# A scan layer and an expert layer on one core: one interleaved loop, or two phases

## The chip, the cores and the metric

The kernel runs on one core of a Trainium2 chip. A core has TensorE (PE, matrix products into PSUM), VectorE (DVE), ScalarE (ACT), GpSimd (POOL) and SyncE (SP, which issues transfers). SBUF is the working memory, PSUM has eight banks of 128 x 512 f32. The metric is the device time of the program in microseconds, the median of several runs. The profile is one further execution.

## What is computed

Input is 16 sequences of 512 tokens with 128 features. Four sublayers follow one another, each with a residual and a layer norm: linear attention, a first expert layer, a state-space layer, and a second expert layer. The change touches the last two only. Cut from the reference:

```python
xz = x @ in_proj_w.T                       # 128 -> 512, split into xi, z of 256
xc = silu(conv4(xi) + conv_b)              # depthwise, 4 taps
xp = xc @ x_proj_w.T                       # dt_raw, B (16), C (16)
dt = softplus(dt_raw * dt_proj_w + dt_proj_b)
dA = exp(dt * A); dBx = dt * xc * B        # for each of 16 states
h_t = dA_t * h_(t-1) + dBx_t               # scan over 512 tokens
y  = sum_n h[n] * C[n] + xc * D
x3 = layernorm(x2 + (y * silu(z)) @ out_proj_w.T)
# second expert layer: 8 experts of 176, top 2, and a shared one, computed densely
h  = silu((x3 @ w1 + b1) * (x3 @ w3 + b3)) * gate
out = layernorm(x3 + h @ w2 + biases)
```

## The kernel before

Stage 1 (attention and routing), the choice of tokens and the first expert layer fill the time up to about 503 us. They are the same in both kernels. After that comes one loop in which every engine runs the same `iteration(f, s, m, o, ahead)`, written out in steps n = 0 to 15, one for each state. Four sequences are in it at a time: `s` is being scanned, `f` (the next one) is being prepared by `front` (normalisation x2, transposition, convolution, projections, softplus), and `m` and `o` (the two before) are in the expert layer, one chunk of 128 hidden units in each step, 13 chunks in all.

A sequence has its 256 channels as two halves of 128 partitions (`NH` = 2), each with 512 tokens, so that a tile of a state is 128 x 1024. For state n:

- TensorE spreads row B of state n over all partitions (`spread_b`, L890), ScalarE copies it to SBUF (`copy_b`, tile bs, L670), and GpSimd multiplies it by u = dt * xc (`spread_u`, tile dbx, L528).
- ScalarE writes the decays (`scan_step`, tile dA, L678), in two SBUF buffers.
- VectorE runs the scan over both halves in one instruction (tile hst, L1330; the first decay of each half is zero) and multiplies by row C, which TensorE has spread into PSUM (`spread_c`, L894; tile prod, L1343).
- TensorE adds the product into PSUM by a product with the identity (`add_state`, L906). For three pairs of states (PAIRS) VectorE adds two products first (L1348).

At the end of a sequence comes yd (the term with D), y2 (the gate), `out_proj` (L949), x3p (the sum with x2) and the normalisation to x3. In the expert part, TensorE runs `hidden` (w1 and w3, L915 and L917), `spread_w` (gates, L922) and `down` (w2, L934); ScalarE makes ha and ht; VectorE hg, hs and hh (`gate`, `silu`, `weigh`).

The order on each engine is the order in which these functions write it. An engine executes in that order, and waits on semaphores: for instance `bb_rdy` counts the spreads of B, `scan_rdy` the scans, `op_mm` the output projections. `s.at(per, k)` is the count that is reached when k of a sequence's `per` events are done.

## Time and profile before

| | |
|---|---|
| median of 3 runs | 2514.21 us (2509.17 to 2514.93) |
| span of the profiled execution | 2515.7 us |
| VectorE busy | 2154.8 us (86%) |
| TensorE busy | 1786.1 us (71%), mean granted clock 0.844 |
| GpSimd busy | 1118.2 us (44%) |
| ScalarE busy | 1035.9 us (41%) |
| first scan starts | 551.64 us |

The span is from the first to the last instruction; it is 1.5 us above the median of the runs. The granted clock is TensorE's, 1.0 being 2.4 GHz and 0.5 being 1.2 GHz. Busy shares are means over stages: the loop is the part from 503 us.

### The profile page before, as it was taken

The numbers are of one execution on the slowest core, as the hardware profiler recorded it, in microseconds if no ns is written. First come the engines' busy times: TensorE is split into PE (matmuls) and PEld (weight loads), VectorE is DVE, ScalarE is ACT, GpSimd is POOL, SyncE is SP. The second block draws the span as 40 slices with busy tenths as digits, with TensorE's granted clock in tenths as the row PEclk, the third lists the DMA queues.
The fourth block names the chain that finished last, engine by engine and source line by source line (L and its number), as shares of the span: only waits on it lengthen the run. The fifth ranks groups of instructions, "written<-read, shape, count | busy, mean of one in ns | idle before, by whom it ended". The sixth has DMA issues, their size and how long they took to land.

```text
span 2515.7 us, 24789 instructions
## 1 busy us (share of the span) xinstructions
PE 1786.1 (71%) x6433; PEld 982.1 (39%) x6433; DVE 2154.8 (86%) x3132; ACT 1035.9 (41%) x1722; POOL 1118.2 (44%) x602
## 2 busy tenths in 40 slices
PE   4776104346787887877787878787878787878687
PEld 3454003312344444444344434443444444444344
DVE  4888791139899998999999999999999999999996
ACT  1322000135463545454545444454545354636343
POOL 1101306724556454554455545555454445454540
PEclk7999555567898889898898888898888889989899
DMA  6333102300000000000000000000000000000000
GB/s 168 100 106 98 27 1 39 37 17 8 5 5 9 5 9 5 8 4 9 5 9 4 9 5 9 4 13 1 13 0 13 1 13 0 13 1 5 5 1 9
DMA packets 72565, 49.75 MB, mean 20 GB/s; under 512 B 5296, under 2 KB 68432, under 8 KB 72144
## 3 DMA queue, kind: packets, MB, share of 16 engines
q1 hardware_dynamic: 57872, 39.85, 5.5%
q0 software_dynamic: 14592, 8.92, 2.8%
q14 instruction: 82, 0.67, 0.1%
q8 instruction: 19, 0.31, 0.1%
HBM read 27.50 MB, written 21.18 MB: 19 GB/s over the span
## 4 chain that ended last, share of the span: by engine, by line
DVE 35%; PE 26%; issue 22%; POOL 11%; ACT 2%; DMA 1%; SPq 1%; DVEq 1%; POOLq 0%; ACTq 0%
DVE hst L1330 8%; PE bank L906 7%; DVE prod L1343 5%; POOL dbx L528 5%; PE bank L915 3%; PE bank L917 3%; DVE prod L1348 3%; DVE hg L1253 3%; PE bank L934 2%; DVE hh L1266 2%; PE bank L949 1%; DVE cand L1154 1%; DVE val L1157 1%; POOL rwp L506 1%; PE bank L862 1%
## 5 line engine op out<-in xcount | busy, mean ns | idle before, releaser
L528 POOL TENSOR_TENSOR dbx<-u,bs 128x1024 f32<-128x1024 f32 x256 | 719.0, 2818 | 363.9 <-ACT bs L670 232.1
L1330 DVE TENSOR_TENSOR_SCAN hst<-dA,dbx 128x1024 f32<-128x1024 f32 x256 | 675.7, 2639 | 26.2 <-issue 14.6
L906 PE MATMUL bank<-prod,ident 128*128 128x512 f32 x832 | 490.3, 720 | 79.3 <-DVE prod L1348 58.0
L678 ACT ACTIVATE dA<-dt,aneg 128x511 f32<-128x511 f32 x512 | 338.2, 709 | 17.3 <-DVE hst L1330 15.2
L1343 DVE TENSOR_TENSOR prod<-hst,bank 128x1024 f32<-128x1024 f32 x256 | 310.4, 1213 | 19.4 <-PE bank L894 11.2
L670 ACT ACTIVATE bs<-bank 128x512 f32<-128x512 f32 x256 | 151.3, 591 | 338.2 <-PE bank L890 335.4
L906 PEld LDWEIGHTS bank<-prod,ident 128*128 128x128 f32 x832 | 183.3, 226 | 258.3 <-issue 154.7
L691 ACT ACTIVATE ht<-hg 128x512 f32<-128x512 f32 (+1 forms) x208 | 130.8, 629 | 309.5 <-DVE hg L1253 308.3
L915 PE MATMUL bank<-x3T,w_w 128*128 128x512 f32 (+1 forms) x416 | 230.1, 636 | 0.7 <-ACT x3T L696 0.7
L894 PE MATMUL bank<-parts,sel_bc 99*128 99x512 bf16 x256 | 107.6, 420 | 166.0 <-DVE prod L1343 164.2
L917 PE MATMUL bank<-x3T,w_w 128*128 128x512 f32 (+1 forms) x416 | 213.9, 596 | 0.1
L1260 DVE SCALAR_TENSOR_TENSOR hs<-ht,hg 128x512 f32<-128x512 f32 (+1 forms) x208 | 198.7, 955 | 3.9 <-ACT ht L691 2.6
L934 PEld LDWEIGHTS bank<-w_w,hh 128*128 128x128 f32 x1408 | 183.9, 191 | 45.6 <-issue 38.4
L1253 DVE SCALAR_TENSOR_TENSOR hg<-bank,w_b,ha 128x512 f32<-128x512 f32 (+1 forms) x208 | 154.4, 742 | 50.3 <-PE bank L917 50.0
L427 POOL TENSOR_SCALAR rs<-mv 128x4 f32<-128x4 f32 x48 | 51.8, 1079 | 327.1 <-DVE mv L1061 327.1
L934 PE MATMUL bank<-w_w,hh 128*128 128x128 f32 x1408 | 185.8, 275 | 0.8 <-DVE hh L1266 0.8
L685 ACT ACTIVATE ha<-bank,w_b 128x512 f32<-128x512 f32 (+1 forms) x208 | 142.4, 684 | 58.7 <-PE bank L915 57.1
L862 PE MATMUL bank<-x2T,inc 128*128 128x512 f32 x256 | 147.9, 720 | 2.3 <-ACT cv L636 1.4
L917 PEld LDWEIGHTS bank<-x3T,w_w 128*128 128x128 f32 (+1 forms) x416 | 79.5, 191 | 112.2 <-issue 110.3
L1266 DVE TENSOR_TENSOR hh<-hs,bank 128x512 f32<-128x512 f32 x176 | 118.5, 673 | 0.0
L915 PEld LDWEIGHTS bank<-x3T,w_w 128*128 128x128 f32 (+1 forms) x416 | 84.3, 208 | 87.1 <-issue 74.6
L890 PE MATMUL bank<-parts,sel_bc 99*128 99x512 bf16 x256 | 111.4, 435 | 8.7 <-ACT bs L670 7.0
(202 smaller groups left out, 2529.6 us busy)
## 6 DMA issues: line engine op xcount, KB each, us to landing
xg_rows<-xg SPq DMA_DIRECT2D x16, 320.0 KB, 2.5
xt<-in_x SPq DMA_DIRECT2D x16, 256.0 KB, 3.1
xT<-in_xT SPq DMA_DIRECT2D x16, 256.0 KB, 3.4
resid_rows<-zero SPq DMA_DIRECT2D x16, 256.0 KB, 3.4
resid_rows<-resid SPq DMA_DIRECT2D x16, 256.0 KB, 2.4
rin<-resid_rows SPq DMA_DIRECT2D x16, 256.0 KB, 2.8
rin<-resid_rows POOLq DMA_DIRECT2D x16, 256.0 KB, 4.8
out_dram<-ofin SPq DMA_DIRECT2D x16, 256.0 KB, 2.4
```

The costliest lines, as they stand in the source:

```text
L528: gp.tensor_tensor(dbx[n % 2][:, :, :], u[s.par][:, :, :], bs[n % 2][:, :].rearrange("p (h t) -> p h t", h=1).to_broadcast([P, NH, SEQ]), ...
L678: act.activation(dA[n % 2][:, h, 1:SEQ], dt_[s.par][:, h, 1:SEQ], ACT.Exp, scale=aneg[:, h, n:n + 1]).then_inc(da_rdy, 1)
L862: last = mm(pv_ps[:, :], inc[:, k, tile(h)], x2T[:, k:k + SEQ], start=(k == 0), stop=(k == DCONV - 1))
L906: last = mm(y_ps[:, h, :], ident[:, :], prod[n % 2][:, h, :], start=(sums_to(n) == 1), stop=(n == NS - 1), skip_group_check=True)
L915: mm(h1_ps[0:k, :], wt["w1"][:, c, 0:k], x3T[:, :], start=True, stop=True).then_inc(h1_mm, 1)
L917: mm(h3_ps[0:k, :], wt["w3"][:, c, 0:k], x3T[:, :], start=True, stop=True).then_inc(h3_mm, 1)
L934: last = mm(fo_ps[:, tile(q)], h[0:k, tile(q)], wt["w2"][0:k, c, :], start=(c == 0 and q == 0), stop=False, skip_group_check=True)
L1253: stt(hg[c % 2][0:k, :], h3_ps[0:k, :], wt["b3"][0:k, c:c + 1], ha[0:k, :], ALU.add, ALU.mult).then_inc(hg_rdy, 1)
L1260: stt(hs[c % 2][0:k, :], ht[c % 2][0:k, :], 1.0, hg[c % 2][0:k, :], ALU.add, ALU.mult).then_inc(hs_rdy, 1)
L1266: tt(hh[c % 2][:, :], hs[c % 2][:, :], pv_ps[:, :], ALU.mult).then_inc(hh_rdy, 1)
L1330: dve.tensor_tensor_scan(flat(hst[n % 2]), flat(dA[n % 2]), flat(dbx[n % 2]), 0.0, ALU.mult, ALU.add).then_inc(scan_rdy, 1)
L1343: tt(prod[n % 2][:, :, :], hst[n % 2][:, :, :], over_h(cb_ps), ALU.mult).then_inc(prod_rdy, 1)
```

## The change

The loop is cut into two. In the first, `iteration(f, s, m, ahead)` has no expert layer: it scans `s`, prepares `f` and closes `m`, and stores x3 of every sequence to DRAM. When all 16 are stored, the second, `experts(nx, s, pv, ahead)`, loads x3 again and runs the 13 chunks of `s` with the routing of `nx` and the end of `pv`. In the first phase, further:

- The decays are written to PSUM, a bank for each half (`da_ps`), and each half has its own scan. On ScalarE `copy_b` and `front` now stand ahead of the decays.
- The normalisations x2 and x3 are ScalarE's (`Identity` with scale and bias for each token); GpSimd computes scale and shift in four operations instead of two.
- The bias of the convolution, the term with D and the residual x2 are added in PSUM by products with a diagonal matrix or the identity; the pairs are gone, so that all 16 states are added by TensorE. xc, zs and y2 are made by VectorE straight from PSUM; the copies cv and zc are gone.
- The softplus sum and the split of xp into three bf16 parts move from VectorE to GpSimd.

In the second phase ha, h1, h3, the gates' bank and ofin are doubled.

```diff
-            def iteration(f, s, m, o, ahead):        # ScalarE
-                    if m and c >= 1:
-                        chunk_t(m, c - 1)
-                    if s and n < NS - 1:
-                        scan_step(s, n + 1)
-                    if s and n < NS - 2:
-                        copy_b(s, n + 2)
+            def decay(s, n):
+                if n == 0:
+                    act.wait_ge(dt_rdy, s.at(1, 1))
+                for h in range(NH):
+                    need(act, scan_rdy, s.at(NS * NH, NH * (n - 1) + h + 1))
+                    act.activation(da_ps[h][:, 1:SEQ], dt_[s.par][:, h, 1:SEQ], ACT.Exp, scale=aneg[:, h, n:n + 1]
+                                   ).then_inc(da_rdy, 1)
+            def iteration(f, s, m, ahead):
+                for n in range(NS):
+                    if s and n < NS - 2:
+                        copy_b(s, n + 2)
+                    if f:
+                        front(f, n)
+                    if m and n == 3:
+                        act.wait_ge(m_rs, m.at(4, 4))
+                        for k in range(TT):
+                            act.activation(x3o[m.par][:, k, :], blk4(pc_ps)[:, k, :], ACT.Identity, ...
+                    if s and n < NS - 1:
+                        decay(s, n + 1)
...
             def front(s, n):                         # ScalarE
+                if n == 0:
+                    act.wait_ge(f_rs, s.at(4, 4))
+                    need(act, op_mm, s.at(1, -1))
+                    for k in range(TT):
+                        act.activation(x2[s.par][:, k, :], rin[s.par][:, k, :], ACT.Identity, bias=nm1[:, k:k + 1],
+                                       scale=rs1[:, k:k + 1]).then_inc(x2_rdy, 1)
...
+            def skip_term(s):                        # TensorE, step 1
+                need(pe, y2_rdy, s.at(1))
+                for h in range(NH):
+                    mm(y_ps[:, h, :], dskip[:, h, :], xc[s.par][:, h, :], start=True, stop=False, skip_group_check=True)
...
+                    if s:                            # VectorE
+                        dve.wait_ge(dbx_rdy, s.at(NS, n + 1))
+                        for h in range(NH):
+                            dve.wait_ge(da_rdy, s.at(NS * NH, NH * n + h + 1))
+                            dve.tensor_tensor_scan(hst[n % 2][:, h, :], da_ps[h][:, :], dbx[n % 2][:, h, :], 0.0, ALU.mult,
+                                                   ALU.add).then_inc(scan_rdy, 1)
...
+            def experts(nx, s, pv, ahead):           # TensorE
+                for c in range(NCH):
+                    if s:
+                        hidden(s, c)
+                    if pv and c < 2:
+                        down(pv, NCH - 2 + c)
+                    if s and c >= SH_CH:
+                        spread_w(s, c)
+                    if s and c >= 2:
+                        down(s, c - 2)
+                    if nx:
+                        prepare(nx, c)
```

On ScalarE, at the start of a sequence (steps 0 and 1 of the repeated part), before: dA is the decay, bs the copy of B, ht and ha the experts' tiles.

```order
L691 ACTIVATE ht0<-hg0 128x512 [waits hs_rdy]
L678 ACTIVATE dA1<-dt0,aneg 128x511 [waits scan_rdy]
L678 ACTIVATE dA1<-dt0,aneg 128x511
L670 ACTIVATE bs0<-bank2 128x512 [waits dbx_rdy]
L685 ACTIVATE ha<-bank4,w_b1 128x512 [waits hg_rdy,h1_mm]
L691 ACTIVATE ht1<-hg1 128x512 [waits hs_rdy]
L678 ACTIVATE dA0<-dt0,aneg 128x511 [waits scan_rdy]
L678 ACTIVATE dA0<-dt0,aneg 128x511
L670 ACTIVATE bs1<-bank2 128x512 [waits dbx_rdy]
```

The same place of the changed kernel: bank2 and bank3 hold the decays, x2_1 is the next sequence's normalised input.

```order
L743 ACTIVATE bs0<-bank5 128x512 [waits dbx_rdy]
L700 ACTIVATE x2_1<-rin1,nm1,rs1 128x128 [waits op_mm]
L700 ACTIVATE x2_1<-rin1,nm1,rs1 128x128 x3
L750 ACTIVATE bank2<-dt0,aneg 128x511 [waits scan_rdy]
L750 ACTIVATE bank3<-dt0,aneg 128x511 [waits scan_rdy]
L743 ACTIVATE bs1<-bank5 128x512 [waits dbx_rdy]
L750 ACTIVATE bank2<-dt0,aneg 128x511 [waits scan_rdy]
L750 ACTIVATE bank3<-dt0,aneg 128x511 [waits scan_rdy]
```

The copy and the normalisation, which waits for `op_mm`, now stand ahead of the decays, and the experts' tiles are gone from here.

On TensorE, steps 1 and 2 of the changed kernel: bank01 is y, bank5 the spread of B, bank4 that of C, bank7 the output projection, bank6 the transposition and the convolution.

```order
L975 MATMUL bank4<-parts0,sel_bc 128x512 [waits prod_rdy]
L980 MATMUL bank01<-xc0,dskip 128x512 [waits y2_rdy]
L985 MATMUL bank01<-prod0,ident 128x512 [waits prod_rdy]
L971 MATMUL bank5<-parts0,sel_bc 128x512 [waits bs_rdy]
L992 MATMUL bank7<-x2_1,ident 128x512 [waits parts_rdy,y2_rdy]
L996 MATMUL bank7<-w_outp,y2 128x128 x8
L932 MATMUL bank6<-ident,x2_1 128x128 [waits dta_rdy]
L932 MATMUL bank6<-ident,x2_1 128x128 x3
L975 MATMUL bank4<-parts0,sel_bc 128x512 [waits prod_rdy]
L985 MATMUL bank01<-prod1,ident 128x512 [waits prod_rdy]
L971 MATMUL bank5<-parts0,sel_bc 128x512 [waits bs_rdy]
L943 MATMUL bank6<-x2T,inc 128x512 x4
```

In the kernel before, the same steps held an expert chunk each; the skip term and the product with x2 were sums on VectorE.

## Rows read from the trace of the kernel before

**Rows 1.** Windows: length, busy us of PE, PEld, DVE, ACT, POOL (instructions), clock, DMA share, GB/s.

```profile
1244.00:1468.00 224.00, 178.32 (x623) 95.80 (x621) 212.54 (x262) 110.05 (x179) 112.91 (x54) 0.88 0.04 7
...
626.00:642.00 16.00, 9.89 (x17) 3.38 (x18) 14.25 (x15) 9.88 (x14) 11.30 (x4) 0.73 0.00 1
...
2482.00:2504.00 22.00, 22.00 (x103) 13.62 (x101) 15.75 (x24) 10.01 (x16) 0.00 (x0) 1.00 0.00 0
```

**Rows 2.** Time line of VectorE (start us, us): the sum `of`, two sequences apart.

```profile
1036.00 0.68 DVE L1315 TENSOR_TENSOR of<-bank,x 128x512 f32<-128x512 f32 x1
...
1279.41 0.68 DVE L1315 TENSOR_TENSOR of<-bank,x 128x512 f32<-128x512 f32 x1
```

**Rows 3.** Groups by line (busy, mean ns, idle before), and instructions' ns min/median/max.

```profile
L1330 DVE TENSOR_TENSOR_SCAN hst<-dA,dbx 128x1024 f32<-128x1024 f32 x256 | 675.7, 2639 | 26.2 <-issue 14.6 <-POOL dbx L528 10.5
...
L1266 DVE TENSOR_TENSOR hh<-hs,bank 128x512 f32<-128x512 f32 x176 | 118.5, 673 | 0.0
...
L1330 DVE TENSOR_TENSOR_SCAN hst<-dA,dbx x256: 2257/2284/4454, 551.6 to 2439.3; 128x1024 f32<-128x1024 f32 x128
...
L1343 DVE TENSOR_TENSOR prod<-hst,bank x256: 1203/1210/1223, 554.0 to 2442.1; 128x1024 f32<-128x1024 f32 x128
```

**Rows 4.** Time lines of VectorE and GpSimd, a scan beside a dbx.

```profile
562.73 3.48 DVE L1330 TENSOR_TENSOR_SCAN hst<-dA,dbx 128x1024 f32<-128x1024 f32 x1
...
561.70 2.36 POOL L528 TENSOR_TENSOR dbx<-u,bs 128x1024 f32<-128x1024 f32 x1 [2.30 <-DVE hst L1330]
```

**Rows 5.** Time line of TensorE, one step at full clock (two records for one f32 product).

```profile
584.78 0.38 PE L894 MATMUL bank<-parts,sel_bc 99*128 99x512 bf16 x1
585.00 1.88 PE L906 MATMUL bank<-prod,ident 128*128 128x512 f32 x4
586.72 0.38 PE L890 MATMUL bank<-parts,sel_bc 99*128 99x512 bf16 x1
```

**Rows 6.** The same at half clock.

```profile
600.59 3.62 PE L906 MATMUL bank<-prod,ident 128*128 128x512 f32 x4
604.00 0.63 PE L890 MATMUL bank<-parts,sel_bc 99*128 99x512 bf16 x1
```

**Rows 7.** TensorE, output projection and the spread behind it.

```profile
1259.92 2.05 PE L949 MATMUL bank<-w_outp,y 128*128 128x128 f32 x16 [2.49 <-DVE hh L1266]
1261.81 0.38 PE L894 MATMUL bank<-parts,sel_bc 99*128 99x512 bf16 x1
```

**Rows 8.** ScalarE: copy and decays in the time line, then groups by line.

```profile
587.13 0.60 ACT L670 ACTIVATE bs<-bank 128x512 f32<-128x512 f32 x1 [2.06 <-PE bank L890]
...
590.01 1.33 ACT L678 ACTIVATE dA<-dt,aneg 128x511 f32<-128x511 f32 x2
...
L665 ACT ACT_TABLE_LOAD x16 | 20.5, 1283 | 0.3
...
L665 ACT ACTIVATE dta<-dta 128x1024 f32<-128x1024 f32 x16 | 16.9, 1057 | 0.2
```

**Rows 9.** TensorE, one chunk of the last sequence, with no scan beside it.

```profile
2484.15 1.02 PE L915 MATMUL bank<-x3T,w_w 128*128 128x512 f32 x2
...
2486.09 1.05 PE L934 MATMUL bank<-w_w,hh 128*128 128x128 f32 x8
2486.98 1.02 PE L915 MATMUL bank<-x3T,w_w 128*128 128x512 f32 x2
```

**Rows 10.** Routing of the last sequence: VectorE's first reduction, TensorE behind GpSimd's split.

```profile
2467.72 0.17 DVE L1289 TENSOR_REDUCE l1z<-l1e 128x4 f32<-128x32 f32 x1
...
2472.39 0.42 PE L969 MATMUL bank<-identb,rwp 128*96 128x128 bf16 x4 [3.40 <-POOL rwp L513]
```

**Rows 11.** VectorE: the first scan, and the last silu.

```profile
551.64 2.29 DVE L1330 TENSOR_TENSOR_SCAN hst<-dA,dbx 128x1024 f32<-128x1024 f32 x1 [3.57 <-POOL dbx L528]
...
2504.57 0.69 DVE L1260 SCALAR_TENSOR_TENSOR hs<-ht,hg 128x512 f32<-128x512 f32 x1
```

More of the change, by code:

```diff
@@ L69, in need @@
     eng.wait_ge(sem, value)
-def sums_to(n):
-    return n + 1 - sum(a < n for a in PAIRS)
 def schedule(eng, iteration):
@@ L564, in _ @@
+            schedule(gp, experts)
         @block.scalar
@@ L869, in front @@
-                if n == 8:
-                    pe.wait_ge(xc_rdy, s.at(1, 1))
-                    turn(pa_ps, xpf_rdy, s.at(1, 1))
+                    else:
+                        need(pe, x3_rdy, s.at(TT, -TT))
+                    to = (pb_ps, pc_ps)[h]
+                    mm(to[:, :], cbias[:, h, :], ones[:, :], start=True, stop=False)
+                    for k in range(DCONV):
+                        last = mm(to[:, :], inc[:, k, tile(h)], x2T[:, k:k + SEQ], start=False, stop=(k == DCONV - 1))
@@ L907, in add_state, with out_proj @@
                               skip_group_check=True)
                 last.then_inc(y_mm, 1)
+            def out_proj(s):
+                pe.wait_ge(y2_rdy, s.at(1, 1))
+                need(pe, parts_rdy, s.at(1, 1))
+                mm(pc_ps[:, :], ident[:, :], x2[s.par][:, :, :].rearrange("p t d -> p (t d)"), start=True, stop=False,
+                   skip_group_check=True)
+                for k in range(TT):
+                    for h in range(NH):
+                        last = mm(pc_ps[:, tile(k)], y2[:, h, tile(k)], wt["outp"][:, h, :], start=False,
+                                  stop=(h == NH - 1), skip_group_check=True)
+                last.then_inc(op_mm, 1)
@@ new lines, in iteration @@
+            def iteration(f, s, m, ahead):
+                for n in range(NS):
+                    if s:
+                        spread_c(s, n)
+                    if m and n == 0:
+                        add_state(m, NS - 1)
+                    if s and n == 1:
+                        skip_term(s)
+                    if s and n:
+                        add_state(s, n - 1)
+                    if s and n < NS - 2:
+                        spread_b(s, n + 2)
+                    if f and n >= NS - 2:
+                        spread_b(f, n + 2 - NS)
+                    if m and n == 1:
+                        out_proj(m)
+                    if f:
+                        front(f, n)
@@ L1030, in _, with experts @@
[L1030 to L1034 removed]
+            def experts(nx, s, pv, ahead):
+                for c in range(NCH):
+                    if s:
+                        hidden(s, c)
+                    if pv and c < 2:
+                        down(pv, NCH - 2 + c)
+                    if pv and c == 1:
+                        biases(pv)
+                    if s and c >= SH_CH:
+                        spread_w(s, c)
+                    if s and c >= 2:
+                        down(s, c - 2)
+                    if nx:
+                        prepare(nx, c)
@@ L1037, in _ @@
+            for done in st_x3:
+                pe.wait_ge(done, ST_ALL)
+            schedule(pe, experts)
         @block.vector
@@ L1366, in _, with experts @@
-            dve.wait_ge(added, E0 // 2 * 16)
-            dve.wait_ge(added2, E0 // 2 * 16)
+                if c == 4:
+                    need(dve, st_o[s.par], s.half(16))
+                    normalise(ofin[s.par], of, mv3, rs3, s, o_rs, ofin_rdy)
+            def experts(nx, s, pv, ahead):
+                for c in range(NCH):
+                    if pv and c == 0:
+                        silu(pv, NCH - 1)
+                        weigh(pv, NCH - 1)
+                    if s:
+                        gate(s, c)
+                        if c:
+                            silu(s, c - 1)
+                        if c - 1 >= SH_CH:
+                            weigh(s, c - 1)
+                    if pv:
+                        finish(pv, c)
+                    if nx:
+                        prepare(nx, c)
```

781 lines of the change are left out of this document (364 added, 417 removed).

## The prediction

> **What bounds the kernel now.** I read the windows first, then the groups by line, then the time lines of all five engines through one sequence. A sequence takes (1279.41 - 1036.00) / 2 = 121.7 us in steady state [rows 2], and in a window of almost two of them VectorE is busy 95% of the time, TensorE 80% at a granted clock of 0.88, ScalarE and GpSimd half [rows 1]. So VectorE is the bound. Part of its time isn't work: a scan of 1024 elements takes 2.26 us at best and 2.64 in the mean [rows 3], and the pair in [rows 4] shows why: GpSimd's dbx runs from 561.70 to 564.06, the scan issued at 562.73 takes 3.48, that is the 1.33 that dbx still needs and a scan. A product that reads PSUM never does this (1.20 to 1.22 over all 256) [rows 3].
>
> **What the change takes from VectorE.** The decays go to PSUM, so the scan has only one SBUF input, as the product has. I take two half scans at the product's behaviour: the fixed part of an instruction is about 0.14 (2 x 0.67 - 1.21, [rows 3]), so a half scan takes 1.21. With the overlap of 0.08 and the drain before a dependent product, a step is 1.13 + 1.24 + 1.14 = 3.51 us. Sixteen are 56.2; the gating and four halves for xc and zs bring it to about 60, before statistics. No trace row has a scan that reads PSUM; if it kept today's mean, a step would be 3.9. The Trainium skill, SBUF — State Buffer, "SBUF: two separate sides", says that a VectorE instruction with two SBUF inputs and a GpSimd instruction take one port pair in turn, for the whole instruction; by that, 0.36 x 256 = 92 us would come back. The trace agrees with the lock, but I don't book the gain, since VectorE isn't the bound of the new first phase.
>
> **What it puts on the path there.** Prices at full clock [rows 5]: a spread 0.22, adding a state (two f32 products of 512 columns, 0.86 each) 1.72; at half clock adding a state is 3.41 [rows 6]. ScalarE starts the copy bs 0.41 after the spread; it takes 0.60, or 0.50 with the next behind it, and a decay half 0.71 [rows 5, 8]. ScalarE's new order is copy_b(n+2), front(n), decay(n+1), and copy_b(n+2) waits for a spread that stands on TensorE behind adding state n-1. So scan(n+1) can't start before product(n-1) ended plus 0.06 + 0.22 + 1.72 + 0.41 + 0.50 + 0.71 + 0.06 = 3.7 us plus what front(n) costs ScalarE. Before, the decays went ahead of the copy into two SBUF buffers, and this path didn't exist. Against 3.5 of VectorE, a plain step is about even; every front operation now shows.
>
> Walked through all 16 steps of a steady period at full clock, the start of each scan against 3.51 after the last:
> Step 1, the largest. ScalarE's first front work, x2 of the next sequence, waits for op_mm of the sequence before (x2 has two buffers), and decay(1) stands behind it. From the end of product(0): gating 1.2 with its latency, skip term 1.72 (0.1 later), state 0 1.72, spread 0.22, the x2 product 0.86 and out_proj 1.89 [rows 7], latency 0.15, four small ACTIVATEs 1.2 (my estimate, from 0.60 for 512 elements), decay 0.71: 9.7 to 9.8 us in which VectorE does the gating only. +9.7.
> Steps 2 to 6. Statistics 1.5. A convolution half is now five products, 4.3 us, on TensorE ahead of the next step's spread_c; xc waits for a tanh queued behind copy_b; z waits for xc; the four x3 ACTIVATEs stand ahead of decay(4). My walk gives +2.8, +5.3, +0.7, +3.0, +1.6 = 13.4.
> Steps 7 to 12. Fronts of 0.2 to 1.35. A front in two neighbouring steps counts once, as the path spans two steps: +3.2.
> Step 13. Two table loads of 1.28 around Ln of 1.06 [rows 8], now ahead of the decay: +3.1. Step 14: statistics, +1.5.
> GpSimd takes over the softplus sum and the split. It has 16 dbx of 2.36 without a wait for the lock [rows 4], u and the sum at the same price, and about ten small operations, some 50 us in all; the sum stands behind Ln in its queue, with dbx(15), u and the next dbx(0) behind it, and by the walk the last of these ends 1 us before its scan is due. The transfers of x3 lie beside the scans. Both at nothing.
> Sum 56.2 + 30.9 = 87.1 us per sequence at full clock. TensorE works 52 of it (16 x 2.16, 1.7, 8.6, 1.7, 2.8, 1.8, 1), with idle of up to 4 us in steps 1, 2 and 14. The stretch of before without experts, 626 to 642, was granted 0.73, a mixture of 1.2 and 2.4 GHz, with the same bursts and gaps [rows 1]. At 1.2 GHz the path of a plain step is 5.8 (adding 3.41, 0.43 more for the two spreads), and as it spans two steps, it costs 4.7 a step instead of 3.6, 1.1 more. I take half of steps 7 to 15 at that clock (+5): 92 us; bounds 87 (never) and 98 (always there, and one convolution).
>
> **The expert phase.** TensorE bounds it: a chunk takes 2.83 us at clock 1.00, its down part 0.89 [rows 1, 9], while VectorE needs three instructions of 0.67 to 0.74. 26 products of 0.86, 13 of 0.89, 11 of 0.22, and biases, transposes and gates of 2.4 make 38.8. Two waits come on top. At chunk 2 down(0) waits for the sum `of`, which VectorE does after gate(2) and silu(1): 2.1. Routing holds VectorE and GpSimd from 2467.72 to 2472.39, 4.7 us [rows 10], behind it hh(8), which spread_w(10) waits for: 2.1. With 1 for the clock after them: 44 us; bounds 42 and 47.
>
> **The sum.** First scan as now at 551.6 [rows 11]; first period without the wait for op_mm 83, 14 x 92 = 1288, last without a front 68; closing the phase (state 15, gating, out_proj, statistics, store) 15; load, transposes and routing with nothing beside them 17; 16 x 44 - 5 = 699 (no routing in the last); end 12.5, as from 2504.57 now to 2515.7 + 1 [rows 11]. 551.6 + 83 + 1288 + 68 + 15 + 17 + 699 + 12.5 = 2734 us of span. Today's profiled span is 2515.7, 1.5 above the median of 2514.2, so **2732**. In short, 121.7 us becomes 92 + 44 = 136: the two parts have different bounds (waits, then TensorE), and before each filled the other's holes.
>
> **The rivals.**
> Forecast, 0.72: as above, slower by 5.5 to 12%.
> TensorE stays at full clock, 0.14: 87 and 43 give 2734 - 14 x 5 - 5 - 16 = 2643. For it: work is denser than in 626 to 642; against it the gaps.
> Half clock through most of the first phase, 0.06: 98 or more and 47, 2870. TensorE: Matmul & The Clock Gate in the Trainium skill, "Part 1: The HAM clock gate", calls the half rate the default that only activity lifts; by it alone every step behind a gap would be slow, and the sum would be this one. The trace agrees in part: the adds from 600.59 are at half rate, those from 585.00 in a denser stretch at full [rows 5, 6].
> Faster, 0.05: the paths through ScalarE hide behind VectorE, so that the phase runs at its 60 plus 3 of statistics. With 44: 551.6 + 16 x 107 + 15 + 17 - 5 + 12.5 = about 2303. It decides where 92 + 44 has fallen to 122.5, 13.5 us per sequence; removing the wait of step 1 alone doesn't do it. Against it: the wait for op_mm and the queue orders are in the rows of the program above.
> Nothing gained, nothing lost (within 0.3%), 0.03: step 1's wait overlaps and the front of steps 3 to 6 costs half: 80 + 42.5, 2515.
>
> The range of 2610 to 2850 holds the forecast's own bounds and most of the second case. A measurement of this kernel tells about 0.3% from no change; slower by more 0.92, within 0.03, faster 0.05.
>
> **What would show it.** Scans at 1.2 us that never vary, and the period of y2 near 92 us; VectorE idle some 8 us before scan(1) with the decay in PSUM as releaser, ScalarE before x2 waiting for L996; ScalarE's bs copies released by L971 in nearly all steps; clock 0.7 to 0.85 in the first phase; in the second, `of` every 44 us, TensorE over 85% busy and its clock above 0.9. I am wrong if the scans in PSUM are slow, if ScalarE is late nowhere, or if the clock stays at one level.

## The result and the profile after

| kernel | median, us (lowest to highest) | ratio to before, 95% interval |
|---|---|---|
| before | 2514.57 (2509.17 to 2596.89; runs beside it) | |
| changed | 2748.41 (2737.57 to 2749.28) | 1.0921, 1.0896 to 1.0946 |

The change makes the kernel 9.2% slower; forecast were 2732 us and a range of 2610 to 2850. The ratios here and below are of fast executions alone, so that before's 2596.89 and the 2610.02 of e3 below don't enter them. The profiled execution, with a span of 2734.8 us, is the fastest of the four of the changed kernel; the other three have 2746.5 to 2747.3. In all tables below, "states" is the time from the first to the last product of a state (L1309, 256 of them), and "experts" the mean distance of the sums `of`; both come from the first and last start that the view by tile shows.

First the windows of the changed kernel (length; busy us of PE, PEld, DVE, ACT, POOL with instructions; clock, DMA share, GB/s): the first phase, one period of it, the second phase.

```profile
555.00:1992.00 1437.00, 991.07 (x2598) 422.64 (x2599) 995.17 (x1075) 661.00 (x1109) 758.04 (x480) 0.89 0.04 8
1284.00:1377.00 93.00, 65.63 (x169) 28.10 (x168) 62.71 (x69) 42.28 (x71) 48.22 (x31) 0.87 0.04 9
...
2035.00:2735.00 700.00, 636.23 (x2987) 390.50 (x2985) 477.09 (x1104) 273.36 (x482) 38.38 (x92) 0.98 0.04 12
```

Before, VectorE was busy 95% of a window [rows 1]. Now no engine is in the first phase: TensorE and VectorE 69% each. In the second, TensorE is busy 91% at clock 0.98. What they wait for in the first phase says the view of waits (engine and line, what it waits for: us in total, times, longest):

```profile
ACT bs L743 <- PE bank L971: 579.7, 219, 7.5
PEld bank L975 <- DVE prod L1309: 440.7, 178, 9.0
PE bank L975 <- DVE prod L1309: 321.5, 161, 8.5
POOL dbx L570 <- ACT bs L743: 294.1, 114, 6.3
DVE hst L1304 <- ACT bank L750: 286.1, 131, 11.5
```

These five close a circle: the copy bs waits for the spread L971 (behind the adding of a state on TensorE; 219 times among 256 copies), the decay L750 stands behind the copy, the scan waits for the decay, TensorE for the product. Now the instructions that answer to [rows 2, 3], by line (ns min/median/max, first and last start):

```profile
L1304 DVE TENSOR_TENSOR_SCAN hst<-bank,dbx x512: 1187/1199/1225, 555.1 to 1989.2; 128x512 f32<-128x512 f32 x171
...
L1309 DVE TENSOR_TENSOR prod<-hst,bank x256: 1220/1220/1222, 557.4 to 1990.5; 128x1024 f32<-128x1024 f32 x128
...
L1393 DVE TENSOR_TENSOR of<-bank,x x16: 674/676/692, 2068.9 to 2727.1; 128x512 f32<-128x512 f32 x16
...
L570 POOL TENSOR_TENSOR dbx<-u,bs x256: 2337/2353/2368, 552.7 to 1984.0; 128x1024 f32<-128x1024 f32 x128
```

The scans no longer vary: the longest of 512 takes 1.23, where before the longest of 256 took 4.45 for twice the elements. The sequences' sums are (2727.1 - 2068.9) / 15 = 43.9 us apart. Two scans of state 1, one period apart, on VectorE's time line:

```profile
1288.64 2.34 DVE L1304 TENSOR_TENSOR_SCAN hst<-bank,dbx 128x512 f32<-128x512 f32 x2 [11.55 <-ACT bank L750]
...
1381.46 2.34 DVE L1304 TENSOR_TENSOR_SCAN hst<-bank,dbx 128x512 f32<-128x512 f32 x2 [10.67 <-ACT bank L750]
```

That is 92.8 us in this period. The mean of 14 periods comes from the gatings (tile y), the first and the last that ends a steady period, on VectorE's time line:

```profile
638.97 1.21 DVE L1295 TENSOR_TENSOR y<-zs,bank 128x1024 f32<-128x1024 f32 x1
...
1928.94 1.21 DVE L1295 TENSOR_TENSOR y<-zs,bank 128x1024 f32<-128x1024 f32 x1
```

(1928.94 - 638.97) / 14 = 92.1 us (single ones from 88.7 to 94.8), and 92.1 + 43.9 = 136.0 where 121.7 was [rows 2]. The largest wait, in the time line of three engines:

```profile
1284.40 1.95 PE L996 MATMUL bank<-w_outp,y 128*128 128x128 f32 x16
1286.38 1.65 ACT L700 ACTIVATE x<-rin,nm,rs 128x128 f32<-128x128 f32 x4 [12.92 <-PE bank L996]
1287.94 1.28 ACT L750 ACTIVATE bank<-dt,aneg 128x511 f32<-128x511 f32 x2
```

ScalarE stands still for 12.92 us until the output projection of the sequence before has read x2, and decay(1) stands behind it. The second place, steps 2 and 3:

```profile
1298.65 3.60 PE L943 MATMUL bank<-x2T,inc 128*128 128x512 f32 x8
1302.08 0.38 PE L975 MATMUL bank<-parts,sel_bc 99*128 99x512 bf16 x1
1304.43 0.60 ACT L743 ACTIVATE bs<-bank 128x512 f32<-128x512 f32 x1 [5.61 <-PE bank L971]
1305.55 0.69 DVE L1285 SCALAR_TENSOR_TENSOR xc<-tc,bank 128x512 f32<-128x512 f32 x1 [1.78 <-ACT tc L709]
```

The convolution stands on TensorE ahead of the spread of C for the next product, all behind it is late, and xc waits for a tanh queued behind the copy.

### The profile page after: what moved, and what is told of

Its sections match the earlier page's. It is cut to its first block, busy times and chain, and to the rows that moved or that the text cites. A ratio compares the mean times of both kernels' runs of the same rounds, so it can differ in the third digit from the quotient of the medians.

```text
span 2734.8 us, 26674 instructions
## 1 busy us (share of the span) xinstructions
PE 1897.1 (69%) x6785; PEld 989.3 (36%) x6785; DVE 1803.5 (66%) x3121; ACT 1038.6 (38%) x1802; POOL 955.9 (35%) x730
## 4 chain that ended last, share of the span: by engine, by line
PE 50%; DVE 21%; issue 13%; ACT 7%; POOL 5%; DMA 1%; SPq 1%; DVEq 1%; ACTq 0%; POOLq 0%
PE bank L985 12%; PE bank L1072 6%; PE bank L1051 6%; PE bank L1053 6%; DVE hst L1304 5%; PE bank L943 4%; DVE prod L1309 3%; PE bank L980 2%; PE bank L975 2%; POOL dbx L570 2%; ACT bank L750 2%; PE bank L948 2%; DVE cand L1219 1%; PE bank L971 1%; DVE val L1222 1%
## 5 line engine op out<-in xcount | busy, mean ns | idle before, releaser
L1304 DVE TENSOR_TENSOR_SCAN hst<-bank,dbx 128x512 f32<-128x512 f32 x512 | 597.8, 1209 | 318.5 <-ACT bank L750 286.1
L570 POOL TENSOR_TENSOR dbx<-u,bs 128x1024 f32<-128x1024 f32 x256 | 601.4, 2353 | 510.8 <-ACT bs L743 294.1
L985 PE MATMUL bank<-prod,ident 128*128 128x512 f32 x1024 | 567.2, 682 | 1.4 <-DVE prod L1309 1.4
L750 ACT ACTIVATE bank<-dt,aneg 128x511 f32<-128x511 f32 x512 | 335.6, 690 | 17.4 <-DVE hst L1304 17.1
L1309 DVE TENSOR_TENSOR prod<-hst,bank 128x1024 f32<-128x1024 f32 x256 | 312.5, 1221 | 44.8 <-issue 32.7
L975 PE MATMUL bank<-parts,sel_bc 99*128 99x512 bf16 x256 | 110.4, 431 | 321.5 <-DVE prod L1309 321.5
L985 PEld LDWEIGHTS bank<-prod,ident 128*128 128x128 f32 x1024 | 227.3, 222 | 203.6 <-issue 192.0
L975 PEld LDWEIGHTS bank<-parts,sel_bc 99*128 99x128 bf16 x256 | 26.6, 104 | 456.4 <-DVE prod L1309 440.7
L1350 DVE SCALAR_TENSOR_TENSOR hs<-ht,hg 128x512 f32<-128x512 f32 (+1 forms) x208 | 141.8, 682 | 5.3 <-PE bank L1072 5.3
L454 POOL TENSOR_SCALAR rs<-mv 128x4 f32<-128x4 f32 x16 | 3.7, 229 | 329.8 <-DVE mv L1126 310.4
L943 PE MATMUL bank<-x2T,inc 128*128 128x512 f32 x256 | 118.8, 608 | 0.0
L1053 PEld LDWEIGHTS bank<-x3T,w_w 128*128 128x128 f32 (+1 forms) x416 | 79.2, 190 | 106.2 <-issue 106.2
```

The source lines that it names most:

```text
L570: gp.tensor_tensor(dbx[n % 2][:, :, :], u[s.par][:, :, :], bs[n % 2][:, :].rearrange("p (h t) -> p h t", h=1).to_broadcast([P, NH, SEQ]), ...
L750: act.activation(da_ps[h][:, 1:SEQ], dt_[s.par][:, h, 1:SEQ], ACT.Exp, scale=aneg[:, h, n:n + 1]).then_inc(da_rdy, 1)
L943: last = mm(to[:, :], inc[:, k, tile(h)], x2T[:, k:k + SEQ], start=False, stop=(k == DCONV - 1))
L975: mm(cb_ps[:, :], sel_bc[:, 1 + NS + n, :], parts[s.par][:, :], start=True, stop=True).then_inc(cb_rdy, 1)
L985: last = mm(y_ps[:, h, :], ident[:, :], prod[n % 2][:, h, :], start=False, stop=(n == NS - 1), skip_group_check=True)
L1053: mm(h3_ps[c % 2][0:k, :], wt["w3"][:, c, 0:k], x3T[s.par][:, :], start=True, stop=True).then_inc(h3_mm, 1)
```

## The experiments

Times are compared by the ratio to before; each kernel was run beside the kernel before. The columns "states" and "experts" come from one execution each. The first phase of e4 is that of the changed kernel, and its states take 1446.5 where 1433.1 stand above: differences of some 13 us in that column are those of one execution from another.

| kernel | us | ratio | states | experts |
|---|---|---|---|---|
| changed | 2748.41 | 1.0921 | 1433.1 | 43.9 |
| e1_x2_kept | 2636.82 | 1.0483 | 1337.6 | 43.9 |
| e2_decays_first | 2626.71 | 1.0454 | 1320.3 | 43.9 |
| e3_both | 2583.14 | 1.0225 | 1286.7 | 43.9 |
| e4_early_sum | 2706.53 | 1.0763 | 1446.5 | 41.5 |
| e5_decays_in_sbuf | 2949.41 | 1.1729 | 1650.4 | 43.7 |
| e6_balanced | 2446.60 | 0.9736 | 1149.3 | 43.9 |
| e7_balanced_all | 2391.34 | 0.9501 | 1149.4 | 40.3 |
| e9_sum_on_vector | 2381.38 | 0.9473 | 1144.5 | 40.3 |
| e10_tensor_filled | 2703.46 | 1.0755 | 1403.2 | 43.9 |
| e8_before_copy_first | 2539.18 | 1.0097 | | |

The theory under test: the first phase is bound by no engine but by a circle through ScalarE's queue order and by the wait for op_mm, and the second by TensorE. The rivals: the PSUM scans, the clock, or the front's own work make the time.

**The wait of step 1.** GpSimd copies x2 to x2k in step 8, the output projection on TensorE adds x2k, and ScalarE waits for the copy before it writes the next x2:

```diff
+                    if s and n == 8:
+                        need(gp, op_mm, s.at(1))
+                        gp.wait_ge(x2_rdy, s.at(TT, TT))
+                        settle(gp)
+                        gp.tensor_copy(x2k[:, :, :], x2[s.par][:, :, :]).then_inc(xk_rdy, 1)
...
-                    need(act, op_mm, s.at(1, -1))
+                    need(act, xk_rdy, s.at(1, -1))
+                    need(act, x2T_mm, s.at(1, -1))
...
-                mm(pc_ps[:, :], ident[:, :], x2[s.par][:, :, :].rearrange("p t d -> p (t d)"), start=True, stop=False,
+                pe.wait_ge(xk_rdy, s.at(1, 1))
+                mm(pc_ps[:, :], ident[:, :], x2k[:, :, :].rearrange("p t d -> p (t d)"), start=True, stop=False,
```

> The changed kernel, but GpSimd copies x2 of the scanned sequence into a tile of its own at step 8, and the output projection adds that copy, so that ScalarE's normalisation of the next sequence no longer waits for op_mm. One copy of 128x512 more on GpSimd. Theory of the queues (the first phase is long because decays stand behind waits on ScalarE): the gap of 10.7 to 11.6 us before scan(1) falls to about 3, some of it comes back before scan(2), which then waits for the spread behind the skip term; 6 to 9 us per period, 92.8 becomes 84 to 87, the time 2620 to 2665. Rival, that TensorE's chain of skip term, states, output projection and convolution sets the time of steps 1 to 6 anyway: the gap only moves to scans 2 and 3, and the time stays above 2710.

Measured 1.0483 (1.0435 to 1.0531), 110 us less, as expected; the mean period falls from 92.1 to 85.3, (1831.56 - 637.07) / 14 by the gatings. The scan's idle time, of which 11.55 and 10.67 stood ahead of scan(1), is now this in the same place of two periods (VectorE's time line):

```profile
1252.00 2.34 DVE L1313 TENSOR_TENSOR_SCAN hst<-bank,dbx 128x512 f32<-128x512 f32 x2 [4.02 <-ACT bank L758]
...
1335.22 2.34 DVE L1313 TENSOR_TENSOR_SCAN hst<-bank,dbx 128x512 f32<-128x512 f32 x2 [2.98 <-ACT bank L758]
```

The wait of the copy for L971 did not go, it grew (from 579.7 to 667 us by the waits): what stays is the circle.

**The order on ScalarE.** The decay of the next state goes ahead of the copy and of the front:

```diff
                 for n in range(NS):
+                    if s and n < NS - 1:
+                        decay(s, n + 1)
+                    if f and n == NS - 1:
+                        decay(f, 0)
                     if s and n < NS - 2:
                         copy_b(s, n + 2)
...
                     if f:
                         front(f, n)
-                    if s and n < NS - 1:
-                        decay(s, n + 1)
-                    if f and n == NS - 1:
-                        decay(f, 0)
```

> The changed kernel with one block moved on ScalarE: decay(n+1) ahead of copy_b(n+2) and of front(n), as before. Nothing else. Theory of the queues: steps 7 to 13 run at VectorE's 3.5 us with no front in them (6 us less), the wait for op_mm moves from scan(1) to scan(2) and loses 3.5 us of scan and product (4 less), steps 3 to 6 keep their round trips through TensorE and lose 2 to 4; in all 11 to 14 us per period, 92.8 becomes 79 to 82, the time 2540 to 2590. Rival, that decays written to one PSUM bank for each half can't be ahead in any order, since they wait for the scan of their own half: the time moves by less than 50 us.

Measured 1.0454 (1.0435 to 1.0472): 117 us less, where 160 to 210 were expected; the period is 84.7, (1820.33 - 635.05) / 14, where 79 to 82 were. The circle is broken (the copy's wait for L971 falls from 579.7 to 132.9 us by the waits), but it was worth less than the walk said, since what it hid shows behind it. The scans' wait for the decay falls from 286.1 to 89.4 us, but their wait for GpSimd's dbx grows from 24.2 to 89.0, that of zs for its tanh from 29.1 to 64.8, and x2 still waits 116.6 us for the output projection (156.4 before the edit).

**Both.**

> Both edits together. If their gains add, as the theory of the queues has it where each removes a wait of its own: 18 to 21 us per period, 92.8 becomes 72 to 75, the time 2450 to 2500, under the kernel before. If TensorE's chain at half clock is what stands behind both, the sum stays at 82 or above, the time above 2580. The theory that the cut into two phases is what costs, whatever the order inside, says that no order brings it under 2514.

Measured 1.0225 (1.0192 to 1.0258): 175 us less (165 by the medians), 52 less than the two gains in sum. So the gains did not add, and 2450 to 2500 is missed; time and period lie where the expectation put the second reading, TensorE's chain at the lower clock. No run separates that reading from the round trips below. For a share of the clock speaks that its executions of 2565, 2579 and 2587 us had mean clocks of 0.892, 0.887 and 0.881. The mean of 14 periods is (1785.38 - 633.75) / 14 = 82.3 us; in the one read step by step, of 78.9 and so one of the shorter ones, plain steps take 3.50, so that VectorE bounds them, and steps 2 to 6 still cost 14.8 on top. VectorE's waits in this phase:

```profile
DVE hst L1313 <- POOL dbx L572: 78.9, 48, 3.6
DVE zs L1299 <- ACT tz L721: 64.4, 30, 2.7
DVE prod L1318 <- issue: 59.2, 24, 3.2
DVE xc L1294 <- ACT tc L717: 53.3, 30, 1.8
```

The second and fourth row are round trips of the front, in which VectorE stands at the head of its queue for a tanh that ScalarE has just begun, 118 us together. The third is the product behind a late spread of C: in 20 of the 24 times the spread ends less than 0.2 us before the product starts.

**The front spread over more steps.** e6 is e3 with the ten products of the convolution in five steps (CONV, on TensorE), tanh and gate of xc in steps 4 and 7 (first pair of conditions, on ScalarE and VectorE) and of z in 6 and 9 (second pair), and, on ScalarE, the front ahead of the copy in steps 2 to 9; x projection, split and dt follow about one step later. The copy x2k moves from step 8 to step 4, and some of these products change their PSUM bank:

```diff
+            CONV = {2: ((0, -1), (0, 0), (0, 1)), 3: ((0, 2), (0, 3)), 4: ((1, -1), (1, 0)), 5: ((1, 1), (1, 2)), 6: ((1, 3),)}
...
-                if n in (3, 5):
+                if n in (4, 7):
...
-                if n in (4, 6):
+                if n in (6, 9):
...
+                    if f and 1 < n < 10:
+                        front(f, n)
```

> e3_both (2583 us, period 78.9: plain steps 3.50, steps 2 to 6 +14.8 in all) with the same operations of the front spread over more steps: the ten convolution products stand 3, 2, 2, 2 and 1 in the steps 2 to 6 on TensorE, where five each stood in 2 and 4 (4.3 us ahead of a spread_c); tc and xc on ScalarE/VectorE at 4 and 7, z at 5/6 and 8/9, the x projection at 7, its split at 8, parts at 10, dt at 10/11; and in steps 2 to 9 ScalarE's front work stands ahead of its copy. Theory A: the extra of steps 2 to 6 is the convolution block ahead of spread_c and two round trips in neighbouring steps, so it falls to some 5 us and the period to 69 to 73: 2583 - 15 x 8 = 2440 to 2500 us. Theory B: TensorE's sum of work sets it (52 us of the period at full clock, more at half), or the round trips only move to the later steps: period 76 to 79, 2540 to 2590 us.

Measured 0.9736 (0.9708 to 0.9763), as theory A had it, and faster than the kernel before. Two scans of state 15 one period apart, then the waits of VectorE:

```profile
1198.61 1.22 DVE L1319 TENSOR_TENSOR_SCAN hst<-bank,dbx 128x512 f32<-128x512 f32 x1 [2.32 <-POOL dbx L572]
...
1270.24 1.22 DVE L1319 TENSOR_TENSOR_SCAN hst<-bank,dbx 128x512 f32<-128x512 f32 x1 [2.33 <-POOL dbx L572]
```

```profile
DVE hst L1319 <- POOL dbx L572: 81.0, 54, 3.7
DVE prod L1324 <- PE bank L987: 47.8, 24, 4.3
```

71.6 us here, and 72.9 in the mean of 14, (1642.66 - 622.29) / 14; the waits for tc and tz are gone. The window of its first phase:

```profile
551.00:1702.00 1151.00, 919.31 (x2598) 414.38 (x2598) 985.33 (x1074) 681.87 (x1108) 766.44 (x492) 0.92 0.05 10
```

VectorE is busy 985 of 1151 us. So the two-phase form is not slow by itself: with the same engines doing the same work but for one copy, 92.1 became 72.9 by the order of the queues. TensorE's clock rose with it: for the same products TensorE is busy 991 us in the changed kernel, 949 in e3 and 919 here, at a clock of 0.89, 0.91 and 0.92. Whether that is a cause of the gain or only follows from the shorter waits, and how much of it, no run shows.

**The expert phase.** At the end of a sequence the changed kernel shows, on VectorE and TensorE:

```profile
2335.91 0.68 DVE L1393 TENSOR_TENSOR of<-bank,x 128x512 f32<-128x512 f32 x1
...
2336.64 1.58 PE L1072 MATMUL bank<-w_w,hs 128*128 128x128 f32 x8 [1.87 <-DVE of L1393]
2338.02 1.91 PE L1051 MATMUL bank<-x3T,w_w 128*128 128x512 f32 x2
```

down(0) waits 1.87 us for the sum `of`. The edit puts the sum ahead of gate(2) on VectorE:

```diff
                 if c == 2:
-                    dve.wait_ge(b2_mm, s.at(1, 1))
-                    tt(of[:, :, :], blk4(fo_ps), x3[s.par][:, :, :], ALU.add).then_inc(of_rdy, 1)
...
+                    if pv and c == 2:
+                        dve.wait_ge(b2_mm, pv.at(1, 1))
+                        tt(of[:, :, :], blk4(fo_ps), x3[pv.par][:, :, :], ALU.add).then_inc(of_rdy, 1)
```

> The changed kernel, second phase only: the sum `of` moves on VectorE from behind silu(1) of chunk 2 to ahead of gate(2), where VectorE is idle. It tells whether down(0)'s wait for it costs what it shows. Priced from the trace: TensorE idles 1.9 to 2.3 us there, and some of the products behind it run at half clock (down(0) 1.4 for 0.9, the products of chunk 3 up to 1.7 for 0.86, 1.8 us in all), so 43.9 us per sequence become 40 to 42 and the time falls by 30 to 60 us. Rival: the wait moves to the wait for hh(8) in the same sequence and nothing falls.

Measured 1.0763 (1.0745 to 1.0781), 42 us less by the medians. The idle time was 1.87, and 43.9 became 41.5, that is 2.4. The rest is the clock: in this sequence the product behind the gap took 1.91 where 1.02 is usual [rows 9], at a clock of 0.59 from 2336.6 to 2340, and over the whole phase TensorE is busy 636.2 us before the edit and 629.7 after it, 0.4 a sequence. e7 has e6, this, and the routing in two parts on VectorE, ahead of the gates of chunks 8 and 9, with the transposition of its weights one chunk later:

> e6_balanced with, in the expert phase, the sum of the previous sequence's output taken ahead of gate(2) on VectorE (e4_early_sum: 42 us less) and the routing of the next sequence cut into two parts on VectorE, ahead of the gates of chunks 8 and 9, with its weight transpose one chunk later. Theory A: both waits of TensorE in that phase go, 43.9 us per sequence becomes 39.5 to 41, so 45 to 75 us under e6_balanced, 2370 to 2450 us: faster than the kernel before (2515). Theory B: only the sum's wait goes (2.6 us x 16 = 42), the second half of routing is as late for hh(8) as the whole was: 38 to 45 us under e6_balanced.

Measured 0.9501 (0.9480 to 0.9522), 55 us less than e6. The window of its second phase shows TensorE busy 97% at clock 1.00:

```profile
1780.00:2390.00 610.00, 593.49 (x2845) 367.05 (x2843) 452.98 (x1055) 256.36 (x457) 37.10 (x88) 1.00 0.04 13
```

40.3 us per sequence, 3.6 less, of which 2.4 were e4's: the other 1.2 are the routing's. TensorE's waits for hh bear this out, 27.8 us in e4 and 11.0 in e7, 1.1 a sequence.

**The decays in PSUM.** ScalarE writes them to an SBUF buffer of each half; order and waits stay:

```diff
-                    act.activation(da_ps[h][:, 1:SEQ], dt_[s.par][:, h, 1:SEQ], ACT.Exp, scale=aneg[:, h, n:n + 1]
+                    act.activation(dA[h][:, 1:SEQ], dt_[s.par][:, h, 1:SEQ], ACT.Exp, scale=aneg[:, h, n:n + 1]
-                            dve.tensor_tensor_scan(hst[n % 2][:, h, :], da_ps[h][:, :], dbx[n % 2][:, h, :], 0.0, ALU.mult,
+                            dve.tensor_tensor_scan(hst[n % 2][:, h, :], dA[h][:, :], dbx[n % 2][:, h, :], 0.0, ALU.mult,
```

> The changed kernel in every respect but one: each ScalarE decay goes to a 128x512 SBUF buffer of its half instead of the PSUM bank, with the same order and waits, so the half scans read two SBUF operands, as the scan of the kernel before did. Changed kernel: 2748 us. Theory A (what the PSUM destination is worth): a half scan issued while GpSimd's dbx of 2.35 us runs shows the rest of it, as in the kernel before (2.26 at best, 2.64 in the mean for 1024 elements, +0.38 per state), so scan times spread from 1.2 to up to 3.5 us. 256 states x 0.2 to 0.4 = 50 to 100 us if all of it stands on the path, 2780 to 2850; dbx itself shows longer records too, where it comes behind a scan. Theory B: VectorE waits for ScalarE and TensorE anyway at steps 1 to 6, so most of the longer scans fall into idle time: within 15 us of 2748. The order of the decays is the same in both, so the waits of bs for L971 (580 us) stay in both.

Measured 1.1729 (1.1707 to 1.1750): 201 us more than the changed kernel, far over both theories. The scans and dbx by line, then a stretch of VectorE and GpSimd:

```profile
L1305 DVE TENSOR_TENSOR_SCAN hst<-dA,dbx x512: 1187/1224/3350, 551.4 to 2203.0; 128x512 f32<-128x512 f32 x171
...
L571 POOL TENSOR_TENSOR dbx<-u,bs x256: 2337/2354/3269, 549.1 to 2196.1; 128x1024 f32<-128x1024 f32 x128
```

```profile
1344.69 2.36 POOL L571 TENSOR_TENSOR dbx<-u,bs 128x1024 f32<-128x1024 f32 x1 [3.68 <-ACT bs L744]
1345.66 3.58 DVE L1305 TENSOR_TENSOR_SCAN hst<-dA,dbx 128x512 f32<-128x512 f32 x2 [1.20 <-ACT dA L751]
1349.33 2.35 POOL L571 TENSOR_TENSOR dbx<-u,bs 128x1024 f32<-128x1024 f32 x1 [0.99 <-DVE hst L1305]
1350.41 2.35 DVE L1305 TENSOR_TENSOR_SCAN hst<-dA,dbx 128x512 f32<-128x512 f32 x1
```

The second scan pair is issued while dbx runs; two halves take 2.34 elsewhere and 3.58 here, about the 1.39 that dbx still needs (it ends at 1347.05) and a pair. The next dbx waits for the end of the scans, which frees its buffer, and the next scan, issued while that dbx runs, takes 2.35 for one half. So dbx and the scans alternate, 2.35 + 2.33 = 4.7, and a step takes 1350.41 - 1345.66 = 4.75 where the changed kernel's plain step takes 3.5. Sixteen such would be 20 us a period; (1650.4 - 1433.1) / 16 = 13.6 came (12.6 by the medians), for some of it fell into waits that were there anyway. The idle time of the scans for the decay hardly fell (286.1 to 256.7). The Trainium skill, SBUF — State Buffer, "SBUF: two separate sides", has a VectorE instruction with two SBUF inputs and a GpSimd instruction take turns at one port pair, for whole instructions; both kernels agree with it, the one without a second SBUF operand (no scan over 1.23) and the one with (up to 3.35). The expectation erred as it carried over 0.38 per state from a kernel whose steps of 7.6 us left dbx room beside the rest.

**The same order in the kernel before**, on ScalarE:

```diff
-                    if s and n < NS - 1:
-                        scan_step(s, n + 1)
-                    if f and n == NS - 1:
-                        scan_step(f, 0)
                     if s and n < NS - 2:
                         copy_b(s, n + 2)
                     if f and n >= NS - 2:
                         copy_b(f, n + 2 - NS)
+                    if s and n < NS - 1:
+                        scan_step(s, n + 1)
+                    if f and n == NS - 1:
+                        scan_step(f, 0)
```

> The kernel before, with one edit on ScalarE: copy_b ahead of the decay of the next state, the order of the changed kernel (its front operations stay where they were). Theory A: the order costs only where a step is short. Here a step lasts 7.6 us, as the expert layer's work stands between the states, and ScalarE is busy half the time, so the decay is done in time all the same: 2507 to 2523 us (within 0.3%). Theory B: the order by itself costs, because the copy waits for a spread that stands behind adding a state on TensorE, in any step that is not idle: up to 1 us per step, 2540 to 2700 us.

Measured 1.0097 (1.0079 to 1.0115), 23 us by the medians: outside theory A's 0.3% and at the foot of B's range. The order costs 1.4 us a sequence here and 7.3 in the changed kernel (e2). That the short step makes the difference is argued, not shown: e2 also moves the front behind the decay, which here stood behind it all along, and here the decays have two SBUF buffers. VectorE's waits in this kernel from 800 to 2400:

```profile
DVE hg L1253 <- ACT ha L685: 49.7, 40, 2.8
...
DVE hst L1330 <- ACT dA L678: 6.0, 2, 3.1
```

It is not the scans that wait for the decays, but the gates of the expert chunks that wait for their biased product (ha), which stands behind the copy in ScalarE's queue, and the copy waits 443.5 us for its spread where it waited 268.4; in the kernel before the gates waited 34.6 us, for TensorE.

**The sum on VectorE.** In e7, the softplus sum goes from GpSimd to VectorE, behind the product of its step:

```diff
-                    if f and n == 13:
...
-                        gp.tensor_tensor(dt_[f.par][:, :, :], dtr[:, :, :], dta[:, :, :], ALU.add).then_inc(dt_rdy, 1)
+                    if f and n == 13:
...
+                        tt(dt_[f.par][:, :, :], dtr[:, :, :], dta[:, :, :], ALU.add).then_inc(dt_rdy, 1)
```

> e7_balanced_all (2391 us, ratio 0.9501 to before) with one operation back where the kernel before had it: the softplus sum of 1024 elements runs on VectorE, behind the product of step 13, and no longer on GpSimd, where it takes 2.35 us in a row of dt, dbx, u, dbx. In e7 VectorE idles for that row 91 us in all (56 times, 2.32 us ahead of scan(14)). Theory A: the row on GpSimd is the bound of the last steps, so the period of 71.6 us loses 2.35 and gains at most 1.2 to 2.3 on VectorE where it was idle anyway: 1 to 2.4 us a period, 15 to 40 us, 2350 to 2376 us. Theory B: the scans only wait for ScalarE's table loads instead: within 8 us of 2391.

Measured 0.9473 (0.9453 to 0.9494) beside 0.9501 for e7: the intervals overlap, and 7 us less by the ratios (10 by the medians) lie nearer to B. The wait only changed its name:

```profile
DVE dt L1332 <- ACT dta L740: 38.8, 15, 2.7
...
DVE hst L1314 <- POOL dbx L572: 22.0, 24, 1.3
```

In e7 the scans waited 91.1 us for dbx; here it is 26.6 in all, 22.0 of it in this window. But VectorE stands 38.8 us at the sum itself, for the Ln behind ScalarE's table load, as long as GpSimd stood at it in e7 (38.9), and works 1.2 us more a sequence. The Ln bounds that place.

**The clock.** At the end of TensorE's part of a step, in the changed kernel:

```diff
+                    if f and n == 12:
+                        pe.wait_ge(dta_rdy, f.at(NH, NH))
+                    if f and n >= 12:
+                        for _ in range(4):
+                            mm(pb_ps[:, :], sel_bc[:, 0, :], parts[f.par][:, :], start=True, stop=True)
```

> The changed kernel (2748 us, ratio 1.0921) with four more bf16 products of 512 columns (0.22 us each at full clock) on TensorE at the end of each of the steps 12 to 15, into a bank that nothing reads then: they do no work of the kernel and stand in gaps of 1.5 to 2.7 us. It prices the half clock of steps 13 to 15 and of the skip term in step 1 (3.43 where 1.9 is the time at full clock). Theory A: with the gaps filled the clock stays at 2.4 GHz there, the skip term and the adds take 1.9, and the period loses 1.5 to 4 us: 2690 to 2725. Theory B: the clock falls in these steps as before, or TensorE is off the path there, so that nothing is gained: within 10 us of 2748, or up to 15 more for the added products.

Measured 1.0755 (1.0732 to 1.0779): 42 us less by the ratios, with more work on TensorE. Skip term and adding of state 0 in the changed kernel:

```profile
1370.84 3.43 PE L980 MATMUL bank<-xc,dskip 128*128 128x512 f32 x4 [0.74 <-DVE y L1295]
1374.07 2.17 PE L985 MATMUL bank<-prod,ident 128*128 128x512 f32 x4
```

and here:

```profile
1358.98 1.98 PE L980 MATMUL bank<-xc,dskip 128*128 128x512 f32 x4 [0.74 <-DVE y L1300]
1360.80 1.88 PE L985 MATMUL bank<-prod,ident 128*128 128x512 f32 x4
```

3.43 is half clock and 1.98 full. That is one period. Of its 16 skip terms the changed kernel runs none at full clock (2.72 to 3.78), e10 nine (1.98; the other seven 2.94 to 3.41). The idle time ahead of scan(1) falls from 10.67 to 8.97, and this period takes 1367.90 - 1279.04 = 88.9; in the one before it the idle time was still 10.61. Over all, states take 30 us less than in the changed kernel's profile, and 43 less than in e4's, which has the same first phase. Where idle time stayed behind the filling, the clock fell all the same: after 3.40 us of it, adding state 14 took 3.62. So theory A holds in size (2703 where 2690 to 2725 were expected), and half clock is a cost on the path of step 1, not only a sign of waits.

## Why the prediction was right, and where it was not

**The sum.** 2732 against 2748 by the median, 16 short, and 2734 of span against 2734.8 of the profiled execution, the fastest of four (2746.5 to 2747.3 in the others). First phase: forecast 83 + 14 x 92 + 68 = 1439, from first to last scan step 555.1 to 1991.7, 1436.6. Closing of it 15, measured 14.1 (1991.7 to 2005.8). Second phase 44 a sequence, measured 43.9. That the span agrees to one us is luck: the terms inside the period missed in both directions, and in e4, with the same first phase, the mean period is 93.1, (1937.98 - 634.43) / 14, and not 92.1.

**The terms of the period** (steady, scan(1) at 1288.64 to 1381.46; each step's time over 3.51):

| term | forecast | measured |
|---|---|---|
| 16 steps of VectorE | 56.2 | 56.2 (scans 1.20, product 1.22) |
| step 1 | 9.7 | 11.9 |
| steps 2 to 6 | 13.4 | 16.7 (2.6, 5.8, 2.0, 2.9, 3.4) |
| steps 7 to 12 | 3.2 | 3.0 |
| step 13, table loads | 3.1 | 3.2 |
| step 14, statistics | 1.5 | 1.4 |
| half clock | 5, in half of steps 7 to 15 | inside steps 1 and 2 |
| sum | 92.1 | 92.9, with 0.5 in step 0 |

**Step 1**: right mechanism (rows above; e1 takes 110 us of time away), 2.2 short. Two sizes were off. The four small ACTIVATEs of x2 take 1.65 and not the estimated 1.2. And the skip term takes 3.43 where 1.72 was forecast, at half clock, with the adding of state 0 behind it 2.17 instead of 1.88; in the period before it was 3.78 and 2.77, and that step 1 is longer by 0.9.

**Steps 2 to 6**: the convolution block and the round trips are the cause, since spreading them (e3 to e6) brings 9.4 us a period back, 82.3 to 72.9. 13.4 was 3.3 short; the adding of state 1 is at half clock (3.60), and that of states 4 and 6 partly (2.51, 2.84).

**The clock**: the term that was misplaced. "I take half of steps 7 to 15 at that clock" put the half clock into the dense stretch. TensorE added states 7 to 12 at full clock (1.88 each), with idle times of 1.0 to 2.4 us ahead of them, and was at half clock for states 13 and 14 (3.43, 3.56, behind 1.98 and 2.68 of idle time), the skip term (3.43, behind 1.72 and 0.74) and state 1 (3.60, behind 3.48). Its clock was forecast as 0.7 to 0.85 for the phase, and it was 0.89. The sum was right by luck: the 5 us that were not there are the 5.5 missing in steps 1 to 6. e10 shows that part of the period is the clock's: 42 us of the whole, 2.6 a sequence. TensorE: Matmul & The Clock Gate in the Trainium skill, "Part 1: The HAM clock gate", calls half rate the default that activity must lift; the rows of this period agree in so far as every half-rate stretch follows an idle time, but not every idle time is followed by one (2.38 us ahead of state 11, added in 1.88), and by that rule alone the phase would have been the rival of 2870.

**At nothing**: the softplus sum on GpSimd. Right for the changed kernel, in which scans wait for dbx only 24.2 us in all (23 times). That cover goes with the other waits: 78.9 us in e3, 81.0 in e6, and then it is Ln on ScalarE that bounds (e9).

**PSUM scans**: "if it kept today's mean, a step would be 3.9" was too low a bound; with both operands in SBUF a step in which dbx and scans alternate costs 4.75, and the kernel 201 us more (e5), not the 92 that today's mean gives. The forecast used the right value. Its reason for booking no gain, that VectorE isn't the bound of the new first phase, does not hold: with VectorE busy 69% the length of the scans is on the path all the same.

**The expert phase**: 2.1 for the sum and 2.1 for routing were forecast, with 1 of clock: 2.4 with its share of clock, and 1.2 (e4, e7). Without both a sequence takes 40.3, with TensorE busy 97% of it at clock 1.00, that is 39.2 of work where 38.8 was counted.

**The rivals**: that faster decides where 92 + 44 has fallen to 122.5 stands: e3 with 82.3 + 43.9 = 126.2 is 3.7 over it, 59 us in sixteen sequences, and is 57 us slower than before (1.0225; 68 by the medians); e6 with 72.9 + 43.9 = 116.8 is 5.7 under it, 91, and 66 us faster. The side is right in both; by e6 the balance lies nearer to 121 than to 122.5. That removing the wait of step 1 alone doesn't do it stands as well (e1, 1.0483). The rival's price, 63 us for a phase hidden behind VectorE, is reached by no kernel here.

**Left open**: what PSUM decays alone would bring to the kernel before. All its eight PSUM banks are in use, so it wasn't tried. Nor was it settled which of steps 2 to 6 each of e6's moves mended, as they were made together, nor how much of the gains of e3 and e6 is TensorE's higher clock.

## What to carry to other kernels

A kernel in two phases has two bounds that add up: compare their sum with the one period of the interleaved kernel before asking how much faster each operation is (92.1 + 43.9 against 121.7). When a step gets shorter, read the queue order again: an instruction that waits for something late, ahead of one that the bound engine needs (copy before decay, x2's wait before decay(1), a convolution block before a spread), costs time in every period. The order of copy and decay alone cost 1.4 us a sequence in steps of 7.6 us; that of copy, front and decay cost 7.3 in steps of 3.5. Gains from such orders don't add, so look for the next wait (110, 117, together 165 to 175); moves of order and one copy took 13% off the changed kernel here, 2748 to 2391, without an instruction made cheaper, though TensorE's clock rose with the shorter waits (0.89 to 0.92 in the first phase).

## What was not expected of the hardware

- Useless products of TensorE made the kernel 1.5% faster (1.0921 to 1.0755), since with them the clock was at 2.4 GHz in nine of 16 skip terms (1.98 instead of 3.43), which others wait for, where it was in none before.
- The lock between VectorE's scans with two SBUF operands and GpSimd's 2.35 us products costs far more in a tight loop than in a loose one: 0.38 us per state before, and in e5 (1734 - 1209) x 2 = 1050 ns, 1.05 us, in the mean of two halves.
- A decay of 511 elements takes ScalarE 0.69 into PSUM (667 to 723 ns) and 0.72 into SBUF (702 to 750) with the same source: 0.03 us, over 512 decays at most 15 of the 201 us.
